# Redone poolings in a graph network: interleaved tanh polynomials, eight search rounds on one joined key, a tie test from the last totals, node rows stored in two parts

## What is computed

```python
def topk_pool(x, w, src, dst, mask, k):
    score = jnp.tanh((x * w).sum(-1) / jnp.sqrt((w * w).sum()))
    _, idx = jax.lax.top_k(score, k)
    ...
    mask2 = mask & kept[src] & kept[dst]
    return (x[idx], new_id[src], new_id[dst], mask2, idx)
...
for i in range(DEPTH):
    x = gcn_conv(x, dn_W[i], dn_b[i], src, dst, mask, n)
    x = jax.nn.relu(bn_train(x, dn_g[i], dn_beta[i]))
    xs.append(x)
    x2, src2, dst2, mask2, idx = topk_pool(x, pool_w[i], src, dst, mask, k)
...
for i in range(DEPTH):
    x = jnp.concatenate([xf, xs[DEPTH - 1 - i]], axis=1)
    x = gcn_conv(x, up_W[i], up_b[i], src, dst, mask, n)
```

## Time and profile before

| | us |
|---|---|
| median of three runs | 1093.03 (1090.64 to 1096.88) |
| span of the profiled execution | 1086.4 |
| TensorE busy | 919.9 |
| VectorE busy | 611.1 |
| ScalarE busy | 404.8 |
| GpSimd busy | 69.5 |

### The profile page before, as it was taken

The page is one execution under the profiler, slowest core; times in us unless marked ns, Lnnn a source line. Parts: engine busy times, 40 slices in busy tenths (PEclk is TensorE's granted clock), DMA queues, the critical chain, the costliest instruction groups (busy, mean ns, idle before and its releaser), DMA issues.

```text
span 1086.4 us, 17543 instructions
## 1 busy us (share of the span) xinstructions
PE 919.9 (85%) x7173; PEld 610.7 (56%) x7173; DVE 611.1 (56%) x1611; ACT 404.8 (37%) x897; POOL 69.5 (6%) x91
## 2 busy tenths in 40 slices
PE   2368999999999999999999887958875776778997
PEld 1256667866655567755755554654434444455655
DVE  5889999977749725542202672644623644535222
ACT  0879999963650102740100312652104401221200
POOL 4000000000000000000000005030033100020000
PEclk9979999999999999999999998989986797889999
DMA  5010000009800020030000026732123100141002
GB/s 161 1 28 2 2 2 1 2 13 398 347 2 1 1 60 2 1 121 1 1 1 1 1 61 232 207 94 104 33 62 92 50 2 0 31 181 63 3 1 61
DMA packets 39455, 65.84 MB, mean 61 GB/s; under 512 B 3605, under 2 KB 27390, under 8 KB 38853
## 3 DMA queue, kind: packets, MB, share of 16 engines
q1 hardware_dynamic: 34302, 45.14, 12.2%
q0 software_dynamic: 4176, 17.86, 5.2%
q10 hardware_dynamic: 886, 1.61, 0.5%
HBM read 28.29 MB, written 36.31 MB: 59 GB/s over the span
## 4 chain that ended last, share of the span: by engine, by line
PE 58%; DVE 27%; ACT 5%; another core or an unknown queue 3%; DMA 3%; issue 3%; POOL 0%; DVEq 0%; ACTq 0%; SPq 0%; POOLq 0%
PE psum L3004 25%; DVE region L1054 7%; PE psum L2525 6%; DVE region L1047 6%; PE psum L2413 6%; PE psum L2754 2%; PE psum L2490 2%; PE psum L2318 2%; PE psum L2951 2%; PE psum L2822 2%; DVE region L1643 2%; PE psum L2343 1%; PE psum L2831 1%; PE psum L2986 1%
## 5 line engine op out<-in xcount | busy, mean ns | idle before, releaser
L3004 PE MATMUL psum<-adj,region 128*128 128x448 fp8e4 (+1 forms) x1200 | 202.6, 329 | 0.1
L3004 PEld LDWEIGHTS psum<-adj,region 128*128 128x128 f16 x1200 | 116.6, 98 | 79.8 <-DVE region L1836 0.5
L2343 PE MATMUL psum<-region 128*128 128x200 bf16 (+2 forms) x1176 | 113.4, 232 | 25.1 <-DVE region L1054 16.8
L2343 PEld LDWEIGHTS psum<-region 128*128 128x128 bf16 x1176 | 94.8, 100 | 59.8 <-DVE region L1054 31.2
L2144 ACT ACTIVATE region<-psum 128x512 fp8e4<-128x512 f32 (+6 forms) x111 | 62.0, 597 | 85.3 <-PE psum L2986 24.6
L3004 PE MATMUL psum<-region 128*128 128x448 fp8e4 (+3 forms) x452 | 82.4, 343 | 12.1 <-DVE region L1836 12.1
L1986 ACT ACTIVATE adj<-psum 128x400 fp8e4<-128x400 f32 x196 | 86.7, 521 | 14.6 <-PE psum L2347 14.0
L2318 PE MATMUL psum<-adj,region 128*128 128x448 fp8e4 x350 | 92.1, 356 | 0.0
L1054 DVE TENSOR_TENSOR region<-iota_key,region 128x1200 bf16<-128x1200 bf16 x147 | 91.2, 673 | 0.0
L1643 DVE CAST region<-psum 128x512 fp8e4<-128x512 f32 (+2 forms) x87 | 47.7, 599 | 77.2 <-remote 29.5
L1047 DVE TENSOR_TENSOR region<-iota_lo,region 128x3072 bf16<-128x3072 bf16 x49 | 85.6, 1747 | 4.7 <-PE psum L2347 4.6
(11 more groups left out here) (375 smaller groups left out, 1278.7 us busy)
## 6 DMA issues: line engine op xcount, KB each, us to landing
both_table<-adj SPq DMA_DIRECT2D x1, 10000.0 KB, 28.7
adj_table<-adj SPq DMA_DIRECT2D x1, 10000.0 KB, 54.7
region<-dk_dram SPq DMA_DIRECT2D x2, 1568.0 KB, 6.2
adj_table<-region SPq DMA_DIRECT2D x1, 2704.0 KB, 9.3
half_table<-region SPq DMA_DIRECT2D x2, 832.0 KB, 5.3
both_table<-region SPq DMA_DIRECT2D x1, 1650.0 KB, 9.3
xs_dram<-nodebuf SPq DMA_DIRECT2D x1, 1600.0 KB, 5.2
nodebuf<-xs_dram SPq DMA_DIRECT2D x1, 1600.0 KB
```

The lines of the kernel that those rows point to most:

```text
L2343: pe.matmul(psum[:, q % BUILD_BANKS, i * KEYS + k0:i * KEYS + k1], hot_lo[:, r, c, j, :, i], hot_key[:, r, c, j, k0:k1, i], start=(n == 0) ...
L3004: last = pe.matmul(psum[:, b if b < BLOCKS else LAST_BANK, 0:width], here[:, t, k, :], rows, start=(t == 0 and k == 0), stop=(t == n_src - ...
```

## The change

It redoes `tanh`, `pick` and the hand-written TensorE order of the poolings:

- `tanh`: numerator and denominator are evaluated in turn. `mark` raises the semaphore without a wait, and an instruction waits only for its own chain. The masks for saturated scores are made in the same gaps, and the subtraction of one from the other too.
- `pick`: constants and copies of older keys come ahead of the scores. The high search keeps its four rounds, but instead of the split the border is multiplied out, and high and low half become one joined number `both`; the low search runs on it, with the same `need`. Eight totals remain of ten. The mask of kept nodes comes straight from a comparison with the last border, before the tie is known. There is no tie if one of the last 16 totals equals `need`. Only then come the value load and the branch, on VectorE behind the copy of the tile counts, on TensorE behind the ranks (`settle`). The tie block repeats mask, tile sums and ranks if it runs.
- Numbering: `place` carries the offset; `found` holds node numbers instead of tile and lane, so that the product has one half and one instruction gives `node_of`. `picks` becomes fp16 and is made in two parts, and TensorE starts on the first part.
- Node rows of level 0 are stored in two parts, tiles 0 to 11 and 12 to 24, the first when three of the seven groups are out.
- Skip sums: other numbers per round; one block of the pass over level 1 (26 sums) becomes a fifth pass, `LATE_SKIP_AT`, ahead of and in the first up layer.

In VectorE's stream the three tie branches stand at instruction rows 676, 852 and 1044 and jump over 20, 66 and 112 rows; now they stand at 675, 852 and 1045 and jump over 28, 74 and 120.

```diff
-                step(v.tensor_tensor(x2, x, x, ALU.mult))
-                step(v.tensor_scalar(p, x2, TANH_P[0], None, ALU.mult))
-                for c in TANH_P[1:-1]:
-                    step(v.scalar_tensor_tensor(p, p, c, x2, ALU.add, ALU.mult))
...
+                p_at = mark(v.tensor_scalar(p, x2, TANH_P[0], None, ALU.mult))
+                q_at = mark(v.tensor_scalar(to, x2, TANH_Q[0], None, ALU.mult))
+                for k, c in enumerate(TANH_P[1:-1]):
+                    dve.wait_ge(dve_step, p_at)
+                    p_at = mark(v.scalar_tensor_tensor(p, p, c, x2, ALU.add, ALU.mult))
+                    dve.wait_ge(dve_step, q_at)
+                    if k < 2:
+                        q_at = mark(v.scalar_tensor_tensor(to, to, TANH_Q[1 + k], x2, ALU.add, ALU.mult))
...
-                    narrow(key_hi, WHOLE_STEPS, step, total)
-                    narrow(key_lo, WHOLE_STEPS, step, total)
-                    v.tensor_tensor(tie[:], psum[:, 7, 1:2], need, ALU.is_gt).then_inc(tie_ready, 1)
...
+                    step(v.scalar_tensor_tensor(wide_base, count, 65536.0, wide_base, ALU.mult, ALU.add))
+                    step(v.scalar_tensor_tensor(both, wide, wide_base, key_lo, ALU.subtract, ALU.add))
+                    for n, size in enumerate(WHOLE_STEPS):
+                        look(both, low_base, n)
+                        if n == 0:
+                            v.memset(exact, 0.0).then_inc(keys_ready, 1)
+                        more_lows(2)
+                        reached()
+                        step(v.scalar_tensor_tensor(low_base, count, float(size), low_base, ALU.mult, ALU.add))
+                    v.tensor_scalar(kept16[:, 0:tiles_here], both, low_base, -offset, ALU.subtract, ALU.is_ge).then_inc(kept_ready, 1)
+                    step(v.tensor_scalar(search[:, 32:32 + FAN], psum[:, 7, 0:FAN], need, 0.0, ALU.is_equal, ALU.add, accum_out=exact))
+                    v.tensor_scalar(tie[:], exact, 1.0, None, ALU.is_lt).then_inc(tie_ready, 1)
...
+                        dve.wait_ge(tile_counted, level + 1)
+                        v.tensor_copy(tile_counts[0:tiles_here, :], psum[0:tiles_here, 6, 64:64 + P]).then_inc(counts_out, 1)
                     dve.wait_ge(tie_ready, level + 1)
                     tied = dve.value_load(tie[0:1, 0:1], min_val=0, max_val=1)
...
+                    for t0, t1, groups in NODE_STORES[lv]:
+                        sp.wait_ge(node_rows_out, before(L_RAW, lv) + groups)
+                        sp.dma_start(to[:, t0:t1, :], node_rows[lv][:, t0:t1, :]).then_inc(nodes_stored, DMA)
-        SKIP_PASSES = ((0, 0, 3, 0), (0, 3, 4, 7), (0, 4, BLOCKS, 0), (1, 0, 4, 0))
+        SKIP_PASSES = ((0, 0, 3, 0), (0, 3, 4, 7), (0, 4, BLOCKS, 0), (1, 0, 3, 0), (1, 3, 4, 3))
+        LATE_SKIP_AT, LATE_SKIP = 5, 18
+        NODE_STORES = (((0, 12, 3), (12, TILES, L_RAW[0])), ((0, LEVEL_TILES[1], L_RAW[1]),))
-            SKIP_AHEAD = (30, 40, 32)
-            SKIP_ROUNDS = ((36, 41, 46, 51, 56, 61, 66, 71, 78, 87), (46, 52, 58, 64, 70, 76, 82, 88, 94, 100), (38, 44, 50, 56, 62, 68, 74, 80, 86, 92))
+            SKIP_AHEAD = (30, 22, 20)
+            SKIP_ROUNDS = ((36, 41, 46, 51, 56, 57, 62, 67), (28, 34, 40, 46, 52, 58, 64, 70), (26, 32, 38, 44, 50, 56, 62, 68))
+            SKIP_PICK = ((70, 72, 77, 86), (73, 75, 78, 86))
+            RAW_AT = {1: (0,), 3: (1,), 4: (2,), 5: (3, 4), 6: (5,), 7: (6,)}
...
+                    pe.wait_ge(picks_ready, before([2] * PACKINGS, below) + k + 1)
```

313 lines of the change are left out of this document (185 added, 128 removed).

## The result

| | kernel before | changed kernel |
|---|---|---|
| median, us | 1091.84 (1089.96 to 1096.88, 4 runs) | 1063.91 (1063.13 to 1065.55, 4 runs) |
| span of the traced execution, us | 1086.4 | 1063.8 |
| mean granted TensorE clock in it | 0.94 | 0.95 |

The account below looks back on a forecast made before the run. Bound: a chain of waits between TensorE and VectorE, in poolings almost all VectorE's small dependent instructions. Terms 8.2 - 0.8 + 9.2 - 1.2 + 8.5 + 1.8 = 25.7 took span 1086.4 to 1060.7; plus 6.6, 1067.3 us; range 1062 to 1074.5.

Parts of the forecast that it names:

- The front and the join: Tanh to first look: 3.4, 3.1 and 2.95 us saved by pooling; between the searches: 2.04, 1.7 and 1.6 saved.
- The end of the first pooling: Last total to node numbers takes 7.7 us; node numbers come 9.0 us earlier, if the store does not hold the gather.
- The store: First pooling: second node-row store lands in 6.8 us and barely holds the first gather, limiting the saving to 8.2 us.
- The second and third pooling: Savings of 9.2 us to the second pooling's node numbers and 8.5 us to VectorE's next instruction in the third.
- What is given back: Skip sums moved behind the picks of the first and second poolings cost 0.8 and 1.2 us.
- the rival's total of 6.6: Behind the picks: VectorE starts a fixed time after the sums, losing 2 + 4.6 us, total time 1071.9; chance 0.20.
- If its late start belongs to the gathers, the cost is 0: Behind the picks: if the gathers set VectorE's late start, the additional skip sums cost nothing.
- The late sums: 26 skip sums put off to the first up layer gain 1.8 us, bounds -1.5 and +2.3.
- The branch did not grow: Rival: VectorE's branch gap grows to 3.62 in the first two poolings, adding 2.7 + 2.4 us, 1072.4; chance 0.10.
- the gaps cost nothing: Rival in the tanh: interleaving gives nothing, costing 6.6 us over three poolings, 1073.9; chance 0.05.
- the tie test did not fire: Rival: the new tie test fires without equal border keys, running the jumped blocks; 1141 if all three; chance 0.03.
- the constant of 6.6: Whole kernel: the profiled execution lies 6.6 us below the median 1093.03; added unchanged to the predicted span.

Follow-up runs that it names:

- e2: Changed kernel with the node rows of level 0 stored in one transfer again: 1065.9 us, ratio 0.9751 to the kernel before.
- e9: Changed kernel with its table of skip sums rewritten to fill TensorE's idle time between totals: 1055.61 us, ratio 0.9676 to the kernel before.
- e8: The changed kernel measured again, unchanged, on another chip: 1064.76 us, ratio 0.9755 to the kernel before.
- e6: Changed kernel with 40 of the 64 skip sums behind the picks left out in the first and second poolings: 1059.24 us, ratio 0.9697.
- e5: Changed kernel with 38 idle matmuls behind the last skip sum of the first and second poolings: 1063.34 us, ratio 0.9738.
- e11: Kernel before with only the new tanh, its two polynomials interleaved: 1083.88 us, ratio 0.9933 to the kernel before.
- e7: Changed kernel with the idle matmuls of e5 and more in other TensorE waits: 1066.65 us, ratio 0.976 to the kernel before.
- e12: Kernel of e9 with idle matmuls behind two poolings' sums, and 24 more before the second pooling's wait for half gathers: 1058.15 us, ratio 0.969.
- e3: Changed kernel without the 18 late skip sums ahead of the first up layer's wait: 1072.28 us, ratio 0.981 to the kernel before.
- e4: Changed kernel with gathers behind the first group held until ScalarE has evicted the skip sums: 1066.7 us, ratio 0.9748.

## Why the prediction was right, and where it was not

**The front and the join.** As computed: 3.57 us against 3.6. The join costs 0.31 instead of 0.22. The 0.15 put in for the two groups of raw rows in round 5 did not come: from its look to the next (631.52 to 633.72) are 2.20 as in the others.

**The end of the first pooling.** Node numbers 7.6 behind the last total (7.7 said). The branch leaves a gap of 0.59 behind the counts, and picks in f16 keep their rate, 1.95 us for both parts against 1.89 in one.

**The store.** This term was mis-sized: 6.8 us from the nearest row, 5.2 measured, so the node numbers decide and the gain is 9.26 instead of 8.2. e2 shows what hangs on it: 3.6 us at the gather, and at most 1 to 2 in the time.

**The second and third pooling.** 9.46 and 8.94 where 9.2 and 8.5 were said; last total to node numbers 6.3 (6.5), to VectorE in the third 6.1 (6.1). The branch was not behind that: in the third the packed sums decide, and e9 shows VectorE free before 3.8.

**What is given back.** This is the step that failed. It asked whether VectorE's late start belongs to the gathers (cost 0) or to the sums (2 and 4.6 at most), and took 0.8 and 1.2. Its own sign of being wrong came: VectorE's first turned tile, 18.4 and 17.6 us behind the first gather before, stands 20.2 and 22.2 behind it. Measured to the half gathers were 2.97 and 3.55 (2.28 and 3.23 in the trace of e8), close to the rival's total of 6.6, but the rival's mechanism is wrong: e6 has the hold end 18.4 us behind the first gather with 24 sums as with 64. What is lost is the head start. Before, TensorE began its turns at 668.87, 14.05 us behind the first gather; in the changed kernel at 664.68, 19.1 behind. TensorE of before:

```profile
668.87 2.06 PE L2822 MATMUL psum<-ident_h,region 128*128 128x128 f16 x24 [4.29 <-issue]
673.08 0.61 PE L2822 MATMUL psum<-ident_h,region 128*128 128x128 f16 x4 [2.15 <-issue]
673.92 16.66 PE L2822 MATMUL psum<-ident_h,region 128*128 128x128 f16 x221 [0.23 <-DVE region L1643]
```

Its long run of turns begins 19.1 behind the first gather (673.92), as that of the changed kernel does. But 28 of the 249 turns that both kernels have here are done by then, worth 2.1 us at the pace of the other 221. That is most of the 2.97 of the first pooling. The rest is the pace of the run, clock included. In e6, where sums are few, turns run in the hold again. What the clock is worth there: TensorE stands still at the end of the hold and runs at half level behind it, and with the clock kept up (e5) the two stretches are 0.6 to 1.2 and 1.9 to 2.2 shorter. "If its late start belongs to the gathers, the cost is 0" overlooked what was done during the wait.

**Between the poolings.** Predicted as 0 and named nowhere: 2.57 us were lost from the half gathers to the second tanh, where no instruction differs. Both kinds have a second trace: e11, like before there, has 65.40 us against 65.38, and e8, the changed kernel again, 66.77 against 67.95. So the loss is there twice, but only 1.39 the second time. Its places in the windows are the longer stretch at half clock behind 708 and the first products of the next layer (1.24 of the 2.57). That the clock causes all of it is read from the traces; e5, e7 and e12 did not isolate it.

**The late sums.** Gain 2.95 where 1.8 was taken and 2.3 was the upper bound. The bound looked at 8 us. e3 shows 14 us at 0.51 without the 18 sums.

**The rivals.** The branch did not grow, the gaps cost nothing, and the tie test did not fire: eight totals, then the place computation.

**The sum and the range.** The time lies 3.4 below the forecast, within the range, and part of that is luck. In the traces the step on what is given back missed 4.5 us (with the stretch between the poolings 7.1), the searches, the late sums and the end of the kernel brought 4.0 more than computed, and the constant of 6.6 covered the rest: with the 0.1 of this trace the same sum would have said 1060.8, below the range. The upper end of the main case, 1071, doesn't follow from its terms either: +3.3 and +2.6 lead to 1073.2.

## What to carry to other kernels

When steps are taken out of a chain, look at what a waiting engine did with the time. Sums that filled TensorE's waits in the old rounds had to go somewhere. With 40 of them fewer behind the picks of each of two poolings the kernel is about 5 us faster (e6). With the whole table rewritten so that they fill the shorter waits between totals (e9) it is 9 faster in the median; the traces place 6.4 of it, and only 2.3 of that behind the picks. Real work in a wait that would otherwise let the clock fall is worth more than its own length (e3: 18 matmuls, 3.1 us of work, 7.5 to 8.4 us of time). Idle matmuls are not: none of those tried gave a gain that the medians show, and with more of them in front of short hand-overs (e7) the kernel was slower than with the first 38 alone (e5). A forecast has to follow a saving to the next thing that starts late, and to the clock behind it.

## What was not expected of the hardware

In these kernels TensorE's results can reach the other engines late while gathers run. Its last sum ends at 656.7 and ScalarE is released at 664.0; in the second pooling 800.3 and 808.5. With all gathers but the first group held (e4) the delay is below 0.1 us. The release is prompt when the sums end 7.6 us (e2) or 3.6 us (e6) behind the first gather. The hold of the first pooling ends 17.6 to 18.5 us behind the first gather in all kernels but e4; in the changed kernel that is 2.5 us behind the end of GpSimd's thirteenth issue (661.5). Not every signal in between is late: e6 had two in time at 12 us. Whether the issuing, its descriptors or the arriving rows hold them was not told apart.

The clock moves as a whole stretch: in e12 work put ahead of it shortened it by 3.4 us and shifted it onto costlier work.
